# Attention kernel on one core: a new order of the first batch's work, with loads and stores on other queues

## The reference

```python
def reference(x, ...):              # x: (4, 1024, 256) f32
    xn = layernorm(x)
    kv_c = xn @ W_kvd + b_kvd       # 64 columns
    q_c  = xn @ W_qd + b_qd         # 192 columns
    k = concat(kv_c @ W_ku + b_ku, rope(kv_c @ W_kr + b_kr))   # 16 heads, 128 + 64
    q = concat(q_c @ W_qu + b_qu,  rope(q_c @ W_qr + b_qr))
    v = kv_c @ W_vu + b_vu
    ctx = softmax(causal(q k^T / sqrt(192))) @ v
    bw = where(weight >= 0, 1, -1) * mean|weight|              # 256 x 256
    return x + ctx @ W_o + b_o + xn @ bw.T + bias
```

## Time and profile before

| | |
|---|---|
| median of 3 runs | 1487.29 us (1485.34 to 1489.63) |
| the profiled execution | 1487.06 us |
| its span in the profile | 1485.3 us |
| busy: TensorE, VectorE, ScalarE, GpSimd | 1416.0, 1155.7, 1204.2, 981.4 us |
| chain that ended last: TensorE's share | 76% |
| first turn of a head on TensorE | 23.56 us |
| first projection of the loop's step 0 | 119.57 us |

### The profile page before, as it was taken

One profiled execution on the slowest core, in us unless ns is written; L12 is line 12 of the kernel. 1 busy time (PEld: TensorE's weight loads), 2 busy tenths in 40 slices (PEclk: granted clock), 3 DMA queues, 4 the chain that ended last, 5 costly groups with the idle time before them and its releaser, 6 DMA issues.

```text
span 1485.3 us, 27605 instructions
## 1 busy us (share of the span) xinstructions
PE 1416.0 (95%) x9849; PEld 1281.7 (86%) x9849; DVE 1155.7 (78%) x2755; ACT 1204.2 (81%) x2553; POOL 981.4 (66%) x553
## 2 busy tenths in 40 slices
PE   3688999999999999999999999999999999999997
PEld 3467899999799989999889998999889999989987
DVE  2465888888677889888677888888677888878888
ACT  2345888899788888899778898889868888888886
POOL 5254777777656777777766777776767677677750
PEclk9778999999999999999999999999999999999999
DMA  8545121222142232211233221222132422211110
GB/s 232 172 138 153 49 76 43 60 61 61 54 111 64 69 89 62 61 54 55 61 72 100 78 86 51 61 61 61 46 74 67 111 61 62 62 46 42 49 30 29
DMA packets 41550, 110.48 MB, mean 74 GB/s; under 512 B 7574, under 2 KB 18119, under 8 KB 41415
## 3 DMA queue, kind: packets, MB, share of 16 engines
q1 hardware_dynamic: 37126, 95.09, 24.1%
q0 software_dynamic: 3232, 12.58, 2.4%
q10 hardware_dynamic: 1056, 1.05, 0.3%
HBM read 48.92 MB, written 13.63 MB: 42 GB/s over the span
## 4 chain that ended last, share of the span: by engine, by line
PE 76%; ACT 8%; POOL 5%; DVE 4%; DMA 3%; issue 2%; SPq 1%; POOLq 0%; DVEq 0%; ACTq 0%
PE turn L1351 14%; PE ring L1296 10%; PE u_ps L1369 7%; PE ring L1328 7%; PE ring L1326 7%; PE ring L1327 7%; PE u_ps L1370 7%; PE o_ps L1389 3%; PE o_ps L1390 3%; ACT probs L693 3%; PE ring L1258 2%; PE ring L1250 2%; PE ring L1309 2%; ACT probs_hi L702 1%; POOL k_rope L301 1%
## 5 line engine op out<-in xcount | busy, mean ns | idle before, releaser
L925 DVE TENSOR_SCALAR_CACHE_REDUCE probs<-ring,c_t 128x1024 f32<-128x1024 f32 (+7 forms) x512 | 413.8, 809 | 105.1 <-PE ring L1328 100.9
L935 DVE TENSOR_TENSOR probs_lo<-turn,probs_hi 128x512 fp32r<-128x512 f32 (+1 forms) x640 | 401.5, 631 | 70.0 <-ACT probs_hi L702 64.8
L702 ACT ACTIVATE probs_hi<-turn 128x512 fp32r<-128x512 f32 (+1 forms) x640 | 350.5, 550 | 113.2 <-PE turn L1351 107.4
L693 ACT ACTIVATE probs<-probs,row_min 128x1024 f32<-128x1024 f32 (+7 forms) x512 | 394.3, 771 | 12.1 <-DVE probs L925 9.6
L1351 PE MATMUL turn<-ident,probs 128*128 128x128 f32 x2304 | 386.2, 275 | 9.6 <-ACT probs L693 7.3
L1351 PEld LDWEIGHTS turn<-ident,probs 128*128 128x128 f32 x2304 | 285.9, 140 | 37.5 <-ACT probs L693 13.4
L1369 PE MATMUL u_ps<-probs_hi,kv_nat 128*128 128x256 f32 x1152 | 314.6, 302 | 0.3 <-DVE probs_lo L935 0.3
L1370 PE MATMUL u_ps<-probs_lo,kv_nat 128*128 128x256 f32 x1152 | 289.3, 281 | 0.0
L1326 PE MATMUL ring<-k_hi,q_hi 128*128 128x512 f32 (+2 forms) x768 | 280.2, 365 | 0.0
L1328 PE MATMUL ring<-k_hi,q_lo 128*128 128x512 f32 (+2 forms) x768 | 264.0, 344 | 0.0
L1327 PE MATMUL ring<-k_lo,q_hi 128*128 128x512 f32 (+2 forms) x768 | 263.4, 343 | 0.0
(11 more groups left out here) (210 smaller groups left out, 2607.8 us busy)
## 6 DMA issues: line engine op xcount, KB each, us to landing
wp<-wp_scratch SPq DMA_DIRECT2D x31, 640.0 KB, 4.2
swapped<-k_rope SPq DMA_DIRECT2D x128, 128.0 KB, 2.3
wv<-wv_scratch SPq DMA_DIRECT2D x31, 512.0 KB, 3.4
swapped<-q_y SPq DMA_DIRECT2D x64, 128.0 KB, 2.3
swapped<-q_x SPq DMA_DIRECT2D x64, 128.0 KB, 2.4
wp_scratch<-wp_parts POOLq DMA_DIRECT2D x7, 640.0 KB, 3.5
x_sb<-in_L_attn_x SPq DMA_DIRECT2D x4, 1024.0 KB, 6.5
k_hi<-qb_kv_hi SPq DMA_DIRECT2D x16, 256.0 KB, 3.7
```

Of the source, the lines that this page charges most:

```text
L693: act.activation(p, p, ACT.Exp, scale=-1.0, bias=row_min[:, r:r + 1], accum_out=row_sum[:, g % 4, w, h:h + 1]).then_inc(exp_ready, 1)
L702: act.activation(probs_hi[:, r % 4, 0:width], turn[r % 2][:, 0:width], ACT.Identity).then_inc(turned_hi, 1)
L925: dve.tensor_scalar(probs_of(g, w, h), ring[slot_of(entry)][:, KEY_COLUMN[qt]:KEY_COLUMN[qt] + keys], c_t[b % 2][:, qt, ds(pair * 2 + h, 1 ...
L935: dve.tensor_tensor(probs_lo[:, r % 4, 0:width], turn[r % 2][:, 0:width], probs_hi[:, r % 4, 0:width].bitcast(F32), ALU.subtract).then_inc ...
```

## The change

Only the prologue and step 0 are changed, but for two details that hold for all batches.

- ScalarE issues the ten bias rows and the second quarter of W_o; GpSimd issues the first quarter of W_o and then waits for x before it issues its other loads. x comes in two halves.
- `qu_b`, `ku` and `vu` are loaded twice, into both halves of the partitions, so `turn_head` has four transposes of 128 rows instead of one and six of 64; a load of heads is seven DMAs instead of four.
- The down projection's order is turned (all batches): first the part with the keys, then `qa`. The stack waits for the first part alone, and signals keys and queries apart. In the first batch the high and low parts are taken straight from `ring`, and the full value is written after.
- SyncE stores the folded parts instead of GpSimd, in its own order among stack, swaps and spread.
- The swap of the first pair's queries goes to a buffer of its own (the room of the FFN weight and the bias rows), so it no longer waits for the rope of the keys.
- The linear part of the first batch is done in step 0, behind the scores of blocks 0 and 1.
- TensorE, ScalarE and VectorE have a new order in the prologue, with single pieces between the folds. GpSimd adds the residual after all rotary columns.
- The scratch of the natural projection lies in `down_a` instead of `xn_t` (all batches), since the linear part reads `xn_t` later.

```diff
-            ("project", 0, QUERY_Y), ("bias", 0, 0), ("linear", 0, 0), ("linear", 0, 1), ("natural", 0, 0), ("natural", 0, 1))
+            ("project", 0, QUERY_Y), ("bias", 0, 0), ("natural", 0, 0), ("natural", 0, 1))
+FIRST_STEP = {(0, 3): (("linear", 0, 0),), (1, 1): (("linear", 0, 1),)}
...
+        def down_part(k):
+
+            return ((down_b, qb_kv_hi, qb_kv_lo, 1), (down_a, qa_hi, qa_lo, 0))[k]
...
+            def first_swaps():
+
+                sp.wait_ge(ffn_step, 6)
+                sp.wait_ge(bias_step, NH + 2)
+                for h, (rows, source) in enumerate(((64, q_x), (0, q_y))):
+                    sp.wait_ge(evacuated, QUERY_X + h + 1)
+                    for a, b in ((rows, rows + 32), (rows + 32, rows)):
+                        sp.dma_start(first_swapped[a:a + 32, :], source[b:b + 32, :]).then_inc(first_swap[h], 16)
+
             def stack(b):
 
-                sp.wait_ge(down_lo, b * 2 + 2)
-                for rows, part in ((slice(0, 64), qb_kv_hi), (slice(64, P), qb_kv_lo)):
-                    sp.dma_start(kv_stack[rows, :].bitcast(F32), part[64:P, :].bitcast(F32)).then_inc(stacked, 16)
-                    sp.dma_start(qb_stack[rows, :].bitcast(F32), part[0:64, :].bitcast(F32)).then_inc(stacked, 16)
+                sp.wait_ge(down_lo, b * 2 + 1)
+                for to, source, signal in ((kv_stack, slice(64, P), keys_stacked), (qb_stack, slice(0, 64), queries_stacked)):
+                    for rows, part in ((slice(0, 64), qb_kv_hi), (slice(64, P), qb_kv_lo)):
+                        sp.dma_start(to[rows, :].bitcast(F32), part[source, :].bitcast(F32)).then_inc(signal, 16)
...
-                for to, source in ((qu_a, W_qu[0:P, heads]), (qu_b, W_qu[P:QC, heads]), (ku, W_ku[:, heads]), (vu, W_vu[:, heads])):
-                    sp.dma_start(to[turn % 2][:, :], source).then_inc(turn_loaded[turn % 2], 16)
+                sp.dma_start(qu_a[turn % 2][:, :], W_qu[0:P, heads]).then_inc(turn_loaded[turn % 2], 16)
+                for to, source in ((qu_b, W_qu[P:QC, heads]), (vu, W_vu[:, heads]), (ku, W_ku[:, heads])):
+                    for rows in (slice(0, 64), slice(64, P)):
+                        sp.dma_start(to[turn % 2][rows, :], source).then_inc(turn_loaded[turn % 2], 16)
+
+            def store_parts(p):
+
+                sp.wait_ge(rope_w_ready, p * 2 + 2)
+                sp.wait_ge(fold_lo, p * 2 + 2)
...
             load_heads(2)
+            store_parts(0)
+            store_parts(1)
+            stack(0)
+            store_parts(2)
             load_heads(3)
-            stack(0)
             swap(0, 0)
+            store_parts(3)
             spread_keys(0)
-            swap(0, 1)
+            first_swaps()
+            for p in range(4, PAIRS):
+                store_parts(p)
             load_wp(1)
...
+            pool.dma_start(wo[:, 0:LOAD_HEADS, :], W_o[0:LOAD_HEADS * P, :].rearrange("(h p) n -> p h n", p=P)).then_inc(wo_loaded[0], 16)
+            pool.wait_ge(x0_loaded[1], 16)
...
             for p in range(3, PAIRS):
                 rope_columns(p)
-                store_parts(p - 1)
-                if p == 5:
-                    residual(0)
-                    pool.wait_ge(residual_ready, NT)
-            store_parts(PAIRS - 1)
+            residual(0)
+            pool.wait_ge(residual_ready, NT)
...
+                dve.scalar_tensor_tensor(out=low[:, :], in0=ring[slot_of(("down", 0, k))][:, :], scalar=b_down[:, part:part + 1],
+                                         in1=high[:, :].bitcast(F32), op0=ALU.add, op1=ALU.subtract).then_inc(down_lo, 1)
...
+            output_bias()
+            rope(dve, 0, range(0, 1))
+            folded_low(7)
+            folded_low(8)
+            rope(dve, 0, range(1, 3))
+            rope(dve, 0, range(3, 4))
+            folded_low(9)
+            bias_leave()
+            rope(dve, 0, range(4, 5))
+            folded_low(10)
+            folded_low(11)
+            rope(dve, 0, range(5, 7))
+            folded_low(12)
+            folded_low(13)
+            rope(dve, 0, range(7, 8))
+            rope(dve, 0, range(8, 9))
+            folded_low(14)
+            folded_low(15)
+            low_keys(dve, 0, 1)
+            low_keys(dve, 0, 0)
             leave("natural", 0, 0)
+            rope(dve, 0, range(9, ROPE_OPS))
             leave("natural", 0, 1)
...
+            turn_head(4)
+            turn_head(5)
+            begin("transpose", 0, 0)
+            fold(3)
+            begin("transpose", 0, 1)
+            fold(4)
+            turn_head(6)
+            begin("down", 0, 0)
+            fold(5)
+            turn_head(7)
+            fold(6)
+            begin("down", 0, 1)
+            fold(7)
+            turn_head(8)
+            turn_head(9)
+            project_pair(0, ROPE_K)
```

More of the change, by code:

```diff
@@ L605, in leave @@
                 elif what == "down":
-                    act.activation((down_a, down_b)[k], full, ACT.Identity, bias=b_down[:, k:k + 1]).then_inc(down_ready, 1)
+                    to, _, _, part = down_part(k)
+                    act.activation(to, full, ACT.Identity, bias=b_down[:, part:part + 1]).then_inc(down_ready, 1)
                 elif what == "natural":
@@ L648, in down_high, with first_down_high, first_down_full @@
             def down_high(b, k):
+                full, high, _, _ = down_part(k)
                 act.wait_ge(down_ready, b * 2 + k + 1)
-                act.activation((qa_hi, qb_kv_hi)[k][:, :], (down_a, down_b)[k], ACT.Identity).then_inc(down_hi, 1)
+                act.activation(high[:, :], full, ACT.Identity).then_inc(down_hi, 1)
+            def first_down_high(k):
+                _, high, _, part = down_part(k)
+                entry = ("down", 0, k)
+                act.wait_ge(ring_full, ITEM[entry] + 1)
+                act.activation(high[:, :], ring[slot_of(entry)][:, :], ACT.Identity, bias=b_down[:, part:part + 1]).then_inc(down_hi, 1)
+            def first_down_full(k):
+                act.wait_ge(down_lo, k + 1)
+                leave("down", 0, k)
             def next_down_high(b, k):
@@ L996, in sequence @@
                     minimum(g, 0)
+                    if g == 1:
+                        leave("linear", 0, 1)
                     if pair == 3:
@@ L1429, in sequence @@
                     weigh_group(g - 1, 2)
+                    if g == 0:
+                        begin("linear", 0, 0)
                     if pair == 6:
@@ L1518, in turn_head @@
                 pe.transpose(to[:, QA], qu_a[source][:, columns], ident[:, :])
-                for half in range(2):
-                    for where, raw in ((QB, qu_b), (VU, vu), (KU, ku)):
-                        mm = pe.transpose(to[:, where][:, half * 64:half * 64 + 64], raw[source][:, columns], ident[0:64, 0:64])
+                for where, raw in ((QB, qu_b), (VU, vu), (KU, ku)):
+                    mm = pe.transpose(to[:, where], raw[source][:, columns], ident[:, :])
                 mm.then_inc(head_turned, 1)
@@ L1556, in _ @@
             turn_head(1)
[L1557 to L1573 removed]
+            fold(0)
+            turn_head(2)
+            fold(1)
+            turn_head(3)
+            fold(2)
+            turn_head(4)
[14 more added lines that the diff above has]
+            project_pair(0, ROPE_K)
+            fold(8)
+            turn_head(10)
+            project_pair(0, QUERY_X)
+            project_pair(0, QUERY_Y)
+            fold(9)
+            turn_head(11)
+            biases()
+            fold(10)
+            turn_head(12)
+            fold(11)
+            turn_head(13)
+            fold(12)
+            turn_head(14)
+            fold(13)
+            turn_head(15)
+            fold(14)
+            fold(15)
             begin("natural", 0, 0)
```

239 lines of the change are left out of this document (123 added, 116 removed).

## The result

The changed kernel takes 1470.69 us (median of 4 runs, 1467.73 to 1471.95), the kernel before 1486.32 us beside it (median of 4, 1482.51 to 1489.63). The ratio is 0.9893, with a 95% interval from 0.9864 to 0.9922. The time lies in the predicted range, but the gain is 15.6 us where 24.9 were forecast. The profiled execution took 1471.56 us, with a span of 1469.8.

A forecast was written before the change was run, and what follows sets the result against it. The prologue was taken as a chain through waits and in-order queues, the steps as bound by TensorE. Prologue - 30.2 us and step 0 + 5.3 gave - 24.9 from 1487.1, so 1462.2 us; case 1457 to 1467, range 1450 to 1474.

The forecast's parts named there:

- Part 1, the loads: Prologue start: 3.15 MB at 276 GB/s, first turn at 15.5 us instead of 23.56; turn 4 waits 2.5 us.
- Rival 2: Loads: only the rows' issue, 3.9 us, is won; start 19.7, turn 4 at 30.2, 1464 or 1468; above 1467: 0.08.
- Part 2: Turn 4 to the first projection: 20.0 us of TensorE plus 0.5 of waits, projection at 49.0 instead of 64.04 us.
- Part 3: Rope and folds: rope 0 at 56.6 us, q_x's swap landed at 66.1, loop start at 89.4.
- rival 3: SP's single queue is the new bound: two stores ahead of the swaps are 8 us; 1470 us, chance 0.20.
- The forecast's own case: Whole kernel: 1457 to 1467 us, chance 0.50.
- The rest of part 3: From 66.1 us: rope 7.4, folds 7.4, low clock 2.6, fold 15 done at 83.5; natural projection 5.93.
- Part 4: Linear part moved into step 0: + 6.9 - 1.6 = + 5.3 us, bounds 2 and 9.
- The sum: Whole kernel: - 30.2 + 5.3 = - 24.9 us against 1487.1, so 1462.2 us.
- Rivals 1 and 4: 1: no waits for swaps in part 3, 1454 us, chance 0.17; 4: stores in one serial loop, 1499 us, 0.03.
- rival 5: Clock: with denser work TensorE stays at 2.4 GHz, 3 us less, within the first case; no chance of its own.

The follow-up runs named there:

- the last experiment: In SyncE's queue the spread of the keys goes behind the stores of pairs 3, 4 and 5, against the kernel with late loads: 1457.95 us, ratio 0.9814.
- the kernel with late loads: Changed kernel with both swaps sooner in SyncE's queue, heads 4 to 7 ahead of w_down, GpSimd's later loads behind its qr scaling: 1458.25 us, ratio 0.982.

## Why the prediction came out so

**Part 1, the loads: right, and worth less than it seemed.** The first turn came at 14.28 us (forecast 15.5), and turn 4 waited for heads 4 to 7 until 31.13 (28.5): 6.4 us and not 2.5. One us of that is a slip of the sum, since 15.5 and 14 are 29.5. The prediction put 8 of its first 15 us down to the start; with the loads as before 2.3 of them were missing at the projection and 1.2 at step 0. Rival 2's start, 19.7, did not come, but its turn 4, 30.2, came even later. The Trainium skill's rule ("DMA: Bandwidth & Descriptors", "Issuing engines are not separate DMA queues"), by which moving DMAs to other engines saves only the issue time, would account for 3.9 us, the rows' issue, of the 9.3 us by which the first turn is sooner. No run shows it to be wrong, because GpSimd's loads were held until x had landed in the same change; how much of the rest is the rows' place in the queue and how much GpSimd's loads, the runs do not tell.

**Part 2: right in its end, partly by luck.** The projection came at 49.73 (49.0). But from turn 4 to it took 18.6 us where 20.5 were counted, 1.0 of the difference because a warm turn with its four transposes took 0.44 us and not 0.7, and this made up for 1.9 of the 2.6 us that turn 4 was late. The stack was issued at 45.25, 4.5 us ahead of the projection and not 7, and still covered its landing.

**Part 3: the step that failed.** The sum let rope wait 7.6 us from the projection and the swap of q_x 2.4 us behind eight issues of 0.6. Measured, the first took 62.18 - 49.73 = 12.45 us: 4.9 too little, because the forecast moved the load of heads behind the stack but did not count its seven issues (51.04 to 56.83 us) ahead of the swap; 4.3 us is the time that k_rope lay ready. Store 2's two issues stand ahead too, but with the stores on GpSimd the swap went out no sooner. From there to q_x's operation it took 13.26 us instead of 9.5: 3.8 too little, because the eight issues from store 3 to q_x's swap took 8.3 us (64.42 to 72.72) and not 4.8, and the landing 2.7 and not 2.4. Together 8.6 us. This was rival 3 in kind (what stands ahead in SyncE's queue), with heads and spread in the place of stores. That its "two stores ahead of the swaps are 8 us" and its 1470 us are what was measured is luck: it had them from the bytes of two stores. The forecast's own case, 1457 to 1467 us, did not come. The prediction counted SyncE's queue at the swap of q_x and not at that of k_rope. The price of 0.6 came from the stack's first issue, with four issues of heads (2.2 us) ahead of it; here the same kind of issue took up to 1.4 us.

**The rest of part 3.** From q_x's operation to fold 15's end 18.1 us (17.4). The folds ran at a granted clock of 0.50; from 77.88 to 91.50 TensorE was busy without a gap, and VectorE for 11.5 us of these 13.6. VectorE waited 2.5 us in that stretch, each time for ScalarE, which waited for TensorE, so that is the most that the lower clock can have cost; the forecast had 2.6 us for the biases and late folds at the low clock. ScalarE waited for no store there. The natural projection took 7.1 us instead of 5.93, at 0.50 where it was 0.58 before, and the reload of wp, issued at 94.58, would by an estimate (4.1 us from issue to landing in the kernel before) have let step 0 start at 99 or so at best.

**Part 4: right in kind.** 4.1 us against 5.3; against the same kernel with the linear part in its prologue 5.0. The wait for q_y is covered as said. But taking the 9 us out of the prologue brought only some 5 there, part of it given back by the clock (0.50 in the folds' stretch, 0.81 with the pieces in it), so the whole move is worth nothing that shows, where the prediction had it at 3 to 4 us.

**The sum.** 0.7 (projection) + 4.9 + 3.8 (swaps) + 0.7 (folds) + 1.3 (natural projection) - 1.2 (step 0) - 0.9 (behind it) = 9.3; 1462.2 + 9.3 = 1471.5, the profiled execution's 1471.56. Rivals 1 and 4 fell: VectorE waited 17.3 us for swaps, and the stores of the last four pairs were issued 4.5 to 6.2 us apart (77.81, 82.35, 88.53, 93.67 us). Of the clock, rival 5, the folds saw the lower level and not the higher one.

What stays open: where the 15.6 us come from. Put back one at a time, the loads cost 0.7 us by the medians, the linear part and GpSimd's stores nothing, and the stack's place 3.4. What the engines' new order, the four whole transposes and the down parts taken from `ring` bring is not shown by a run, nor what parts put back together would cost. Also, the first start is not divided between the bias rows' queue and GpSimd's wait for x, and whether the last 2.5 us of the spread's move are real would need more runs.

## What to carry to other kernels

Where one in-order queue issues everything, write down for every wait that a compute engine has on a DMA what stands ahead of that DMA in its queue, and what its issue costs while the queue is full; a transfer that somebody waits for goes ahead of one that is needed later, even if the latter has been ready for longer. An earlier start is worth what is left of it at the next late transfer: follow it from wait to wait before it is put into a sum. And when a wait goes, look for the next one at once (here: stack, swaps, stores, reload), since each of them had hidden the following.

## What the runs showed of the hardware

Queues took turns by packets and not by bytes. In the changed kernel from 16 to 20 us, while turn 4 waited, the DMA queues were (packets, MB, share; q0 is GpSimd's, q1 SyncE's, which carried w_down and the heads):

```profile
q0 software_dynamic: 240, 0.78, 88.8%
q1 hardware_dynamic: 236, 0.10, 14.9%
```

The Trainium skill, "DMA: Bandwidth & Descriptors", "Queues, rings and completion order", says that each DMA engine goes round the queues that have work, a packet at a time; the trace agrees, with 240 packets beside 236, and SyncE's queue moved 0.10 MB of 0.92. With GpSimd's later loads issued later and the heads ahead of w_down it moved 0.29 MB in the same 4 us, and turn 4 came 5.9 us sooner.

The issue of a DMA has no fixed price. On SyncE one took 0.32 or 0.43 us after a pause in the queue (store 4 at 64.95 us in the last experiment) and 1.2 or 1.3 us right behind store 3 and the spread (the same store at 67.11 us in the kernel with late loads). Transfers of other queues count too: the seven issues of the heads took 5.8 us in the changed kernel and 9.1 where the store ahead of them ran on GpSimd's queue. Each such DMA holds up what its engine has queued behind it.
